# First attention: the value products move to another PSUM bank, the keys are converted earlier, and two casts go

## What is computed

```python
x = x + jnp.tanh(g_xattn[0]) * _L0_xattn_ref(_layernorm(x, axis=-1), ctx_1024, ctx_1024, ...)
x = x + jnp.tanh(g_ffn[0]) * _L0_ffn_ref(_layernorm(x, axis=-1), ...)
# _L0_xattn_ref
qh = _split(q @ w_q + b_q, B, L)
kh = _split(k @ w_k + b_k, B, L)
vh = _split(v @ w_v + b_v, B, L)
scores = jnp.einsum('bhqd,bhkd->bhqk', qh, kh) * scale
attn = jax.nn.softmax(scores, axis=-1)
out = jnp.einsum('bhqk,bhkd->bhqd', attn, vh)
# _L0_ffn_ref
logits = xf @ Wg.T + bg
probs = jax.nn.softmax(logits, axis=-1)
tp, ti = jax.lax.top_k(probs, K)
```

## Time and profile before

| | |
|---|---|
| median of three runs | 1344.31 us (1343.42 to 1347.88) |
| the profiled execution | 1347.85 us, its span 1346.1 us |
| TensorE busy over the span | 1280.9 us, 95% |
| VectorE, ScalarE, GpSimd busy | 927.0, 805.5, 747.9 us (69%, 60%, 56%) |
| chain that ended last, by engine | PE 86%, DVE 5%, DMA 3%, ACT 2%, issue 2% |

### The profile page before, as it was taken

The page is one execution under the profiler, slowest core; times in us unless marked ns, Lnnn a source line. Parts: engine busy times, 40 slices in busy tenths (PEclk is TensorE's granted clock), DMA queues, the critical chain, the costliest instruction groups (busy, mean ns, idle before and its releaser), DMA issues.

```text
span 1346.1 us, 38344 instructions
## 1 busy us (share of the span) xinstructions
PE 1280.9 (95%) x14758; PEld 1143.9 (85%) x14758; DVE 927.0 (69%) x2426; ACT 805.5 (60%) x1794; POOL 747.9 (56%) x836
## 2 busy tenths in 40 slices
PE   7999999997999999999999988999999998899898
PEld 6888888886899999999999977899999997555476
DVE  3899999997576566555555027999999997221386
ACT  3676776663666777777676435666666665332453
POOL 1377777765478777777876034566666643100231
PEclk8999999998999999999999989999999999999999
DMA  5665554543667676777766811631111110599811
GB/s 173 214 223 192 189 168 165 190 166 108 231 214 217 223 223 220 226 232 228 218 220 224 327 44 29 236 116 49 49 49 56 56 32 29 215 430 429 322 64 64
DMA packets 103892, 237.52 MB, mean 176 GB/s; under 512 B 8992, under 2 KB 86176, under 8 KB 91296
## 3 DMA queue, kind: packets, MB, share of 16 engines
q1 hardware_dynamic: 97568, 218.29, 47.1%
q0 software_dynamic: 6144, 16.79, 3.9%
HBM read 174.22 MB, written 60.82 MB: 175 GB/s over the span
## 4 chain that ended last, share of the span: by engine, by line
PE 86%; DVE 5%; DMA 3%; ACT 2%; issue 2%; SPq 0%; POOL 0%; DVEq 0%; ACTq 0%; PEldq 0%; POOLq 0%
PE ps L1640 13%; PE psT L1625 6%; PE ps L648 6%; PE psS L625 5%; PE ps L802 5%; PE ps L852 5%; PE psT L634 4%; PE ps L661 4%; PE psS L1625 3%; PE ps L1625 3%; PE ps L785 2%; PE ps L815 2%; PE ps L742 2%; PE psT L640 2%; PE ps L1878 2%
## 5 line engine op out<-in xcount | busy, mean ns | idle before, releaser
L1593 POOL TENSOR_TENSOR wb_lo<-arena,wb_hi 128x2048 fp32r<-128x2048 f32 x64 | 298.0, 4657 | 96.7 <-ACT wb_hi L1713 96.7
L1640 PE MATMUL ps<-wb_hi,hT_hi 128*128 128x256 f32 x528 | 152.0, 288 | 2.5 <-DVE hT_lo L1766 2.5
L634 PE MATMUL psT<-arena 32*128 32x128 f32 x2048 | 151.2, 286 | 0.4 <-ACT arena L955 0.4
L1640 PE MATMUL ps<-wb_lo,hT_hi 128*128 128x256 f32 x528 | 149.3, 283 | 0.0
L1640 PE MATMUL ps<-wb_hi,hT_lo 128*128 128x256 f32 x528 | 148.4, 281 | 0.0
L625 PE MATMUL psS<-arena 32*128 32x256 f32 x1024 | 142.8, 397 | 1.2 <-ACT arena L955 0.5
L1713 ACT CAST wb_hi<-arena 128x1024 fp32r<-128x1024 f32 x128 | 130.6, 1045 | 11.3 <-DMA arena<-w_dram 10.7
L634 PEld LDWEIGHTS psT<-arena 32*128 32x128 f32 x2048 | 126.5, 189 | 1.1 <-issue 0.6
L1236 POOL TENSOR_TENSOR arena<-arena,eps_sb 128x1 f32<-128x1 f32 x96 | 23.8, 248 | 164.7 <-DVE arena L1113 114.2
L1778 DVE TENSOR_TENSOR arena<-ps,arena 128x512 f32<-128x512 f32 (+1 forms) x39 | 25.4, 650 | 117.4 <-PE ps L1640 77.0
L625 PEld LDWEIGHTS psS<-arena 32*128 32x128 f32 x1024 | 95.2, 191 | 9.9 <-issue 6.7
(11 more groups left out here) (400 smaller groups left out, 3920.5 us busy)
## 6 DMA issues: line engine op xcount, KB each, us to landing
arena<-wset_dram SPq DMA_DIRECT2D x24, 2048.0 KB, 14.5
xs_rows<-arena SPq DMA_DIRECT2D x33, 1024.0 KB, 5.0
arena<-w_dram SPq DMA_DIRECT2D x32, 1028.0 KB, 6.0
arena<-w_dram SPq DMA_DIRECT2D x32, 1024.0 KB, 5.9
arena<-w_dram SPq DMA_DIRECT2D x7, 2052.0 KB, 13.5
w_sb<-xs_rows SPq DMA_DIRECT2D x33, 256.0 KB, 2.7
xs_rows<-arena SPq DMA_DIRECT2D x33, 256.0 KB, 5.6
arena<-ctxT_dram SPq DMA_DIRECT2D x63, 128.0 KB, 2.3
```

The costliest lines, as they stand in the source:

```text
L634: nc.tensor.matmul(psT[:, b, j * P:(j + 1) * P], kbd[p, (k - 1) % 3, c, par, :], qT[p, (k - 1) % 3, c, :], start=j == 0, stop=False, skip_ ...
L1593: nc.gpsimd.tensor_tensor(wb_lo[:, u % 2, part], wb_raw[:, u % 2, part], wb_hi[:, u % 2, part], ALU.subtract).then_inc(w_g.sem, 1)
L1640: last = nc.tensor.matmul(ps[5][:, t * D:(t + 1) * D], hp[:, f, t * P:(t + 1) * P], wp[:, f, :], start=f == 0 and t == 0 and n == 0, stop= ...
```

## The change

The value products of layer 0's attention are written to the upper half of bank 5, behind the turned rows that lie in its lower half, instead of the upper half of bank 6. ScalarE converts the keys as soon as the key products are done; it waits for the value products only ahead of the values. TensorE waits for the copy of the turned rows ahead of the value products, for the converted keys (no more the values) ahead of the query products, and for the converted values ahead of the gate products, whose columns lie where the values were. VectorE compares the chosen indices in `idx8` themselves with the expert numbers, and writes the row numbers as integers from the reduction; the cast to `top_idx`, the cast from `slot_f`, the two tiles and the steps "keep" and "slot" go. Layer 1's attention keeps its order.

```diff
-        top_idx = sb("top_idx", [P, B, 2])
         idx8 = sb("idx8", [P, 8], U32)
-        slot_f = sb("slot_f", [P, 2])
...
-                rk_v = track(n + "rk_v", "oh both pos run ohp slot put")
-                rt_v = track(n + "rt_v", "lg top idx keep")
+                rk_v = track(n + "rk_v", "oh both pos run ohp put")
+                rt_v = track(n + "rt_v", "lg top idx")
...
                         keys(k + 1, 6)
-                        values(k + 1, 6)
+                        if A:
+                            pe.wait_ge(pre_a.sem, pre_a.at(k + 1, "xT"))
+                        values(k + 1, 5 if A else 6)
...
                         if A and k + 1 >= early:
-                            pe.wait_ge(kv_a.sem, kv_a.at(k + 1, "V"))
+                            pe.wait_ge(kv_a.sem, kv_a.at(k + 1, "K"))
...
+                        if k + 1 >= early:
+                            pe.wait_ge(kv_a.sem, kv_a.at(k + 1, "V"))
                         for c in range(C):
                             last = nc.tensor.matmul(ps[5][:, D:D + E0], xT[:, c, :], wc[:, c, :], start=c == 0, stop=c == C - 1)
...
-                        act.wait_ge(kv_p.sem, kv_p.at(kv(k + 1), "V"))
+                        act.wait_ge(kv_p.sem, kv_p.at(kv(k + 1), "K" if A else "V"))
                         before(act, st_p.sem, st_p.at(k - 2, "b"))
                         keys(k + 1, 6)
+                        if A:
+                            act.wait_ge(kv_p.sem, kv_p.at(k + 1, "V"))
                         before(act, av_p.sem, av_p.at(k - 2, "av"))
-                        values(k + 1, 6)
+                        values(k + 1, 5 if A else 6)
...
-                        dve.wait_ge(rt_v.sem, rt_v.at(sl_i, "keep"))
-                        nc.vector.tensor_tensor(oh2, top_idx[:, sl_i, :, None].to_broadcast([P, 2, E0]),
+                        dve.wait_ge(rt_v.sem, rt_v.at(sl_i, "idx"))
+                        nc.vector.tensor_tensor(oh2, idx8[:, 0:2, None].to_broadcast([P, 2, E0]),
...
-                        nc.vector.tensor_reduce(slot_f[:, :], ohp2, AX, ALU.add).then_inc(rk_v.sem, 1)
-                        dve.wait_ge(rk_v.sem, rk_v.at(sl_i, "slot"))
-                        nc.vector.tensor_copy(slot_i[:, :, sl_i], slot_f[:, :]).then_inc(rk_v.sem, 1)
+                        with nc.allow_low_precision(reason="each sum has a single whole number"):
+                            nc.vector.tensor_reduce(slot_i[:, :, sl_i], ohp2, AX, ALU.add).then_inc(rk_v.sem, 1)
...
-                        dve.wait_ge(rt_v.sem, rt_v.at(rt_i, "idx"))
-                        nc.vector.tensor_copy(top_idx[:, rt_i, :], idx8[:, 0:2]).then_inc(rt_v.sem, 1)
```

## The result

| | before | after | ratio, 95% interval |
|---|---|---|---|
| measured together, 11 runs each | 1348.79 us (1342.83 to 1351.28) | 1339.0 us (1331.9 to 1343.87) | 0.9935 (0.9912 to 0.9958) |
| the profiled execution, its span | 1347.85, 1346.1 us | 1341.84, 1340.1 us | |
| one steady turn of the first attention | 9.22 us | 8.86 us | |
| the 27 equal turns (4 to 30) | 248.96 us | 239.77 us | |

The change makes the kernel faster by 0.65%, 0.42 to 0.88. The forecast was 1333.3 us; 1339.0 stands at the upper end of the range, 5.7 above. The steady turns moved by what was forecast. Two things did not: the level of the kernel before, which was 1348.79 here and not the 1344.31 of the three runs shown (these are among the eleven; the eight others have a median of 1349.2), and what lies behind the first attention, where the profiled execution gave back half of its gain.

The account below looks back on a forecast made before the run. The prediction took TensorE's work plus one hand-over at line 802 to set the turn. Steady turns 9.2, first turns 1.5 and stage end 0.3 sum to 11.0 us, from 1344.31 to 1333.3 us, range 1330.7 to 1339.2.

Parts of the forecast that it names:

- so it moves as a whole: Routing and experts behind the first attention start by semaphores, so they keep the stage's whole gain.
- for the median I forecast 1333.3: Whole kernel: gain of 11.0 us taken from 1344.31, the median of the runs shown.
- The hole: TensorE's wait at line 802 for converted keys and values, 0.37 us a turn; the change closes it.
- the hole has another cause: Rival: line 802 is held by something the change leaves; only first turns and tail move, 1342.5 us; chance 0.08.
- What is late next: Line 840's waits for ScalarE's line 1021 and VectorE's line 1165 cost 0.03 a turn, leaving 0.34 us gain.
- The new waits: Value products wait for ScalarE's row copy, gate products for converted values; costed at 0 (0 to 0.02).
- The casts: VectorE's lines 1188 and 1146 left out: worth nothing directly in steady turns; they make room.
- That would not fit in 8.88: VectorE with the casts needs about 9.13 us of a turn, more than the new turn's 8.88.
- the lower bound: VectorE's need without the casts, 8.46 us a turn if GpSimd's hold isn't passed to line 1198; otherwise up to 8.71.
- First turns: First attention's examples 1 to 4 gain 0.6, 0.6, 0.3 and nothing; sum 1.5 us (0.5 to 2.2).
- End of the stage: After example 31 the chain goes over to VectorE, where leaving out casts gains 0.3 us (0.2 to 0.5).

Follow-up runs that it names:

- casts_only: Changed kernel with bank, moved waits and early key conversion put back, only VectorE's two casts left out; 1348.14 us, ratio 1.0025 to the kernel before.
- handover_only: Changed kernel with VectorE's two casts and their steps put back, the rest of the change kept; 1334.36 us, ratio 0.9921 to the kernel before.
- bank_only: Changed kernel, but ScalarE again waits for the value products ahead of converting the keys; 1343.94 us, ratio 0.9976 to the kernel before.
- late_copy: Changed kernel with ScalarE's copy of the turned rows put between the second and third piece of the key conversion; one run, 1379.69 us.
- after_again: The changed kernel once more, no edit, for a second profile; 1337.41 us, ratio 0.9939 to the kernel before.
- after_fourth: The changed kernel once more, no edit, for a fourth profile; 1334.56 us, ratio 0.9909 to the kernel before.
- lone_early: Changed kernel with the lone expert units' tables made ahead of the first tokens; 1333.82 us, ratio 0.9918 to the kernel before.
- after_third: The changed kernel once more, no edit, for a third profile; one run, 1335.69 us.

## Why the prediction was right, and where it was wrong

What failed are the last steps of the sum, not those on the turn: "so it moves as a whole", which put what a run loses behind the stage at nothing, and "for the median I forecast 1333.3", which took three runs for the kernel's level. The term for the casts was mis-sized as well, which the forecast time doesn't feel. One after the other:

*The hole.* Right in place and size. The chain lost 0.13 + 0.24 us at line 802; the key conversion begins 0.70 earlier in the turn, as forecast. `casts_only` keeps the hole, `handover_only` closes it, so its cause is the hand-over. That rules out the rival "the hole has another cause".

*What is late next.* The step with line 840 held: line 1005 moved from 5.85 to 5.53 in the turn (0.32, forecast 0.33), and line 840's load from 7.79 to 7.45. The turn gained 0.36 us, where 0.34 was forecast, and the 27 turns 9.19, where 9.2 was. That these agree so closely is partly luck: 27 x 0.36 would be 9.7, but turn 4, the first of the 27, still takes 9.17 in `after`. My later expectation for `bank_only` forgot this step: it took line 840 to have slack, which the prediction's own numbers denied.

*The new waits.* Cost 0, as forecast; `late_copy` shows the full price of lateness.

*The casts.* "That would not fit in 8.88" was a mis-sized term: VectorE with the casts takes 8.93, not 9.13. I had taken the idle time ahead of line 1155 from the turn and counted the rest as need. But held time is no fixed need. VectorE's busy time between 100 and 280 us (stretch, us; busy time and count; clock, DMA share, GB/s), before and in `handover_only`, which has the same instructions on it:

```profile
100.00:280.00 180.00, 167.34 (x569) 1.00 0.54 180
...
100.00:280.00 180.00, 168.83 (x584) 1.00 0.56 186
```

That is 8.57 a turn of 9.22, and 8.42 a turn of 8.97, the mean of that stretch. The mechanism (VectorE becomes the pace if the casts stay) was there, at 0.07 us over the turn of 8.86 instead of 0.25 over 8.88. The need without the casts, 8.62, lies within the forecast bounds 8.46 and 8.71. The hold did not pass to the next instruction (line 1199, 208 ns), and still the lower bound was not reached. Part of that is line 1073, which rose from 159 ns on the mean (as line 1069) to 269. It takes 0.16 us in 12 of the 20 turns and 0.43 to 0.44 in the 8 others, where it begins in the first half of GpSimd's extra subtraction of line 1349 and ends with it, as here:

```profile
116.32 0.73 POOL L1349 TENSOR_TENSOR wb_lo<-arena,wb_hi 128x256 fp32r<-128x256 f32 x1
116.66 0.43 DVE L1073 TENSOR_TENSOR arena<-idx,const 128x16 f32<-128x16 uint32 x1
```

So it is the place in the turn, and not the type of the indices, that makes it longer.

*First turns.* In profiles whose granted clock is 1.00 there (`casts_only` against `after_again`), the start of turn 2 moved by 0.97 us, turn 2 shrank by 0.50 and turn 3 by nothing: 1.5, as forecast. The sum was luck: example 1 gave 0.9 of it and example 2 next to nothing, where 0.6 each was expected. Three more profiles with that clock there (`after_fourth`, `handover_only`, `lone_early`) give 1.1, 1.6 and 1.6, within 0.5 to 2.2. The 12.35 us of the first pair of profiles hold more than the change: the clock was at 0.50 to 0.97 from 20 to 36 us before, and down to 0.50 from 20 to 32 after.

*End of the stage.* 0.3 us can't be read: from the last gate product to the first turning of the experts' tokens the profiles take 39.0 to 44.8 us, whichever kernel it is: 39.4 and 43.7 before, and 41.0, 43.4, 41.0 and 41.0 after, the same mean of 41.6.

*"So it moves as a whole."* This step failed for the profiled execution. From 12.35 earlier at the stage's end it came to 6.0 at the span's. What follows starts by semaphores, but how VectorE's tables meet GpSimd's subtractions (0.8 to 6.1 us of idle TensorE) and where the clock falls differ from run to run by as much as the change brings. As a mean it isn't refuted: the spans are 1346.1 and 1344.5 before, 1340.1, 1331.3, 1333.9 and 1334.9 after, whose means lie 10.3 apart, with only two of the six executions before.

*The level.* The other step that failed is "for the median I forecast 1333.3". The kernel before has medians of 1348.79, 1344.45, 1345.61 and 1346.02 in four batches, and single runs from 1338.68 to 1359.55; three runs within 4.5 us of each other said too little of that. A start from the profiled execution, 1347.85, would have been better: the prediction's own 1336.9 for it is 2.1 from 1339.0. Of the 5.7 us between 1333.3 and 1339.0, 1348.79 - 1344.31 = 4.5 is this level and 11.0 - 9.8 = 1.2 the gain, which by medians was 9.8, 7.0 and 11.5 in the three batches. The forecast ratio, 1336.9 / 1347.85 = 0.9918, lies within all three measured intervals of the change (0.9935, 0.9939 and 0.9909 as centres), near the edge of two. One sum of the range is off by a rounding: 1338.2 + 0.9 is 1339.1, not 1339.2.

What stays open: whether the second hold in the experts' stage comes oftener with the change, and what sets the new turn. The chain names TensorE alone, but line 842's load comes exactly as ScalarE releases it; a kernel in which one of the two is shorter was not tried. No kernel was run either with the early conversion and the values left in bank 6, where ScalarE would read while TensorE writes; what the move to bank 5 adds by itself is argued and not shown.

## What to carry to other kernels

When a chain shows a hole, ask what else is released at the same moment: a wait further on can have the same price, and an edit that removes only the first gives nothing (`bank_only`: 9.21 us instead of 9.22). Here the edit that paid was at the producer, ScalarE's earlier start, where all that queues behind it moves along. A gain in one stage of a long program is compared by that stage's time in the traces, and the whole by ratios measured together, not by a difference from a few runs.

## What the runs showed of the hardware

A VectorE instruction of six numbers on one partition took 4.43 us beside a GpSimd subtraction of 4.53, and 0.22 without; small size is no protection. A VectorE instruction of 128x16 took 0.43 us when it began in the first half of a GpSimd subtraction of 0.73, and 0.16 otherwise. The granted clock fell to 0.5 for some 3 to 20 us at places that differ between profiles of one kernel: 20 to 32 us in `after` and `after_third`, nowhere near there in `after_again` and `after_fourth`.
